# Two transformer layers on one core: the first head group of layer 0 laid out over TensorE's row groups, with q's split and the bias loads moved to other engines

## The reference

```python
x_norm = modulate(_ln(x), shift_a, scale_a)
qkv = x_norm @ W_qkv + b_qkv                 # b_qkv: 3 x 128
q, k, v = split(qkv)                         # 16 heads of 8 channels
attn_w = softmax(einsum('bhqd,bhkd->bhqk', q, k) * 8 ** -0.5)
attn_out = einsum('bhqk,bhkd->bhqd', attn_w, v)
...
x = x + gate_a * (attn_out @ W_proj + b_proj)
```

## Time and profile before

| | us |
|---|---|
| median of 3 executions | 492.45 |
| lowest and highest of them | 485.8, 495.92 |
| the profiled execution's own time | 483.93 |
| its span, first to last instruction | 482.2 |
| PE busy | 401.5 (83%) |
| DVE busy | 302.2 (63%) |
| ACT busy | 203.7 (42%) |
| POOL busy | 110.4 (23%) |

### The profile page before, as it was taken

One profiled execution on the slowest core, in us unless ns is written; L12 is line 12 of the kernel. 1 busy time (PEld: TensorE's weight loads), 2 busy tenths in 40 slices (PEclk: granted clock), 3 DMA queues, 4 the chain that ended last, 5 costly groups with the idle time before them and its releaser, 6 DMA issues.

```text
span 482.2 us, 9026 instructions
## 1 busy us (share of the span) xinstructions
PE 401.5 (83%) x3343; PEld 225.6 (47%) x3343; DVE 302.2 (63%) x1282; ACT 203.7 (42%) x302; POOL 110.4 (23%) x131
## 2 busy tenths in 40 slices
PE   3899999999998987989979897987674667675886
PEld 2436531223333225767655646773353444454454
DVE  4743663599999507466453725123988999997332
ACT  1120132466664774566723122431443555553411
POOL 5411030940001012000121400001434344444010
PEclk9855575699999999999989777555757777876989
DMA  7443144011000000000000000000000000000000
GB/s 194 33 152 93 50 145 133 16 50 52 2 2 1 2 0 1 2 2 1 1 0 1 3 3 6 5 3 0 2 1 2 1 2 0 2 1 1 1 24 22
DMA packets 11357, 12.22 MB, mean 25 GB/s; under 512 B 2335, under 2 KB 9713, under 8 KB 11313
## 3 DMA queue, kind: packets, MB, share of 16 engines
q1 hardware_dynamic: 10237, 10.96, 7.7%
q0 software_dynamic: 320, 0.34, 0.9%
q10 hardware_dynamic: 756, 0.34, 0.6%
HBM read 8.75 MB, written 2.62 MB: 24 GB/s over the span
## 4 chain that ended last, share of the span: by engine, by line
PE 58%; DVE 28%; ACT 6%; issue 5%; POOL 1%; DMA 1%; SPq 0%; ACTq 0%; DVEq 0%; POOLq 0%
PE psum L1515 5%; PE psum L1445 5%; PE psum L1483 5%; PE psum L1439 4%; DVE mx L1163 4%; PE psum L1468 3%; DVE left L1235 3%; DVE left L1242 3%; PE psum L1614 3%; PE psum L1306 3%; PE psum L1462 3%; PE psum L1498 3%; DVE top L1232 2%; PE psum L1526 2%; DVE top L1239 2%
## 5 line engine op out<-in xcount | busy, mean ns | idle before, releaser
L1163 DVE TENSOR_REDUCE mx<-psum 128x1 f32<-128x512 f32 x128 | 81.8, 684 | 38.3 <-PE psum L1445 22.4
L765 ACT ACTIVATE big<-psum 128x1024 f32<-128x1024 f32 x64 | 62.5, 1022 | 45.5 <-PE psum L1468 27.3
L575 POOL TENSOR_TENSOR rstd<-vareps,minus_half 128x4 f32<-128x4 f32 x12 | 12.2, 1020 | 191.2 <-DVE vareps L930 191.1
L1515 PE MATMUL psum<-kblk,qf 128*128 128x308 f32 x128 | 48.7, 515 | 1.1 <-DVE qf L1112 0.8
L1445 PE MATMUL psum<-KS,QS 72*128 72x512 bf16 x112 | 44.2, 429 | 3.4 <-DVE mx L1163 2.6
L1526 PE MATMUL psum<-ident,pr 128*77 128x128 f32 x256 | 39.1, 303 | 9.1 <-POOL pr L689 8.9
L1526 PEld LDWEIGHTS psum<-ident,pr 128*77 128x77 f32 x256 | 35.3, 170 | 17.3 <-POOL pr L689 12.2
L689 POOL TENSOR_TENSOR pr<-pr,early 128x616 f32<-128x616 f32 x16 | 23.9, 1493 | 56.5 <-ACT early L870 39.3
L1483 PE MATMUL psum<-big,V 128*9 128x512 f32 x256 | 36.0, 636 | 0.5 <-ACT big L765 0.5
L1538 PE MATMUL psum<-QS,vc 77*9 77x128 f32 x256 | 14.2, 348 | 23.2 <-ACT QS L880 23.1
L1468 PE MATMUL psum<-QS,KS 75*128 75x512 bf16 x112 | 33.1, 383 | 0.4
(11 more groups left out here) (205 smaller groups left out, 710.5 us busy)
## 6 DMA issues: line engine op xcount, KB each, us to landing
QS<-scr_q SPq DMA_DIRECT2D x7, 288.0 KB
KS<-scr_k SPq DMA_DIRECT2D x7, 288.0 KB
scr_q<-qp SPq DMA_DIRECT2D x2, 384.0 KB, 2.5
scr_k<-kp SPq DMA_DIRECT2D x2, 384.0 KB, 3.1
early<-in_L_xcond_w_ada_dram SPq DMA_DIRECT2D x1, 576.0 KB, 5.1
scr_k<-kp SPq DMA_DIRECT2D x2, 256.0 KB, 3.2
wmlp<-in_L_xcond_W_mlp_dram SPq DMA_DIRECT2D x2, 256.0 KB, 3.2
wm<-in_L_xcond_w_m_dram SPq DMA_DIRECT2D x1, 512.0 KB, 4.6
```

Source lines behind the costliest of these rows:

```text
L765: freed(act.activation(pT[:, u % 2, 1024 * half:1024 * (half + 1)], ps, ACT.Exp), "sT", 0, u, half)
L1163: freed(dve.tensor_reduce(mx[:, n % 3, NT * hh + q:NT * hh + q + 1], ps, AX_X, ALU.max), "max", t, q)
L1515: last = pe.matmul(ps[:, 512 * a:512 * a + HH // 2 * S], qf[:, b, i * P:(i + 1) * P], kb[:, c0:c0 + HH // 2 * S], start=True, stop=True)
```

## The change

- **Maxima of the first group.** A step t < 4 used to be head t with its four query tiles, all four from the same 8 partitions. Now it is query tile t of the four heads, each on its own row group and with all 32 rows of it. `mx` gets its columns in the order that fits. The scores of the group take all 32 rows too.
- **Blanks.** For this the rows behind the 8 channels must not disturb: `vecs` is zeroed first (DVE, with the semaphore s_vz on which the loads of the vectors wait), L1_b_qkv is moved to row 32 of it, and the 1 of row 8 is taken out of the q bias (two small memsets of `vecsF`).
- **q's parts.** DVE keeps one operation of five per batch (qf from PSUM). ACT makes the first and second bfloat16 part (`q_first`, `q_mid`), POOL the two differences. They stand in ACT's and POOL's lists between those of k.
- **Bias rows.** All ten `load_wide` copies are issued by ACT, one after the other, right behind half_tanh; none by POOL. There is one semaphore for all.
- **Order.** `mod_columns(0, 1)` moves from before the first maximum to behind "ln" of step 0, and its room from W0 ahead of the steps to the second turn of the W rooms; `ln_norm(0, 1)` moves from before Q0's copy to behind q's; `mod_out(0, 1)` moves from step 0 to step 1, `q_out(1)` from 1 to 2.

```diff
-EARLY_ROOMS = {"ln": (("W", ("lnT", 0, 1)),), ...
+EARLY_ROOMS = {"ln": (("W", ("lnT", 0, 1)), ("W", ("mods", 0, 1))), ...
-                  ("L1_b_ada", 9), ("L1_b_qkv", 3), ("L1_b_q", 1), ("L1_b_kv", 2), ("L1_b_m1", 8)):
+                  ("L1_b_ada", 9), ("L1_b_m1", 8), ("L1_b_q", 1), ("L1_b_kv", 2), ("L1_b_qkv", 3)):
+    _at = QUAD if _name == "L1_b_qkv" else _at
...
         def load_vecs(eng, loaded, *names):
+            eng.wait_ge(s_vz, 1)
...
@@ split_k (POOL)
                 pool.tensor_tensor(res[:, b, 1, :], kf[:, b, :], kp[:, b, 0, :], ALU.subtract).then_inc(s_kres[b], 1)
+                pool.wait_ge(s_qhi[b], 1)
+                pool.tensor_tensor(res[:, b, 0, :], qf[:, b, :], qp[:, b, 0, :], ALU.subtract).then_inc(s_qres[b], 1)
                 pool.wait_ge(s_kmid[b], 1)
                 pool.tensor_tensor(kp[:, b, 2, :], res[:, b, 1, :], kp[:, b, 1, :], ALU.subtract)\
                     .then_inc(s_parts[b], 1)
+                pool.wait_ge(s_qmid[b], 1)
+                pool.tensor_tensor(qp[:, b, 2, :], res[:, b, 0, :], qp[:, b, 1, :], ALU.subtract)\
+                    .then_inc(s_parts[b], 1)
...
-            load_wide(pool, 5, 6, 7, 8, 9)
...
-            load_wide(act, 0, 1, 2, 3, 4)
+            load_wide(act, *range(len(WIDE)))
...
@@ ACT, layer 0, each b
                         k_out(b)
+                        q_first(b)
                         k_mid(b)
+                        q_mid(b)
...
@@ q_out (DVE)
-                dve.tensor_scalar(qf[:, b, :], ps, cols_dh[:, c:c + 1], SCALE, ALU.add, ALU.mult)
-                freed(dve.tensor_scalar(qp[:, b, 0, :], ps, cols_dh[:, c:c + 1], SCALE, ALU.add, ALU.mult),
-                      "qkv", 0, b, "q")
-                wait_read(dve, "qkv", 0, b, "q")
-                dve.tensor_tensor(res[:, b, 0, :], qf[:, b, :], qp[:, b, 0, :], ALU.subtract).then_inc(s_qsplit[b], 1)
-                dve.wait_ge(s_qsplit[b], 1)
-                dve.tensor_copy(qp[:, b, 1, :], res[:, b, 0, :]).then_inc(s_qsplit[b], 1)
-                dve.wait_ge(s_qsplit[b], 2)
-                dve.tensor_tensor(qp[:, b, 2, :], res[:, b, 0, :], qp[:, b, 1, :], ALU.subtract)\
-                    .then_inc(s_parts[b], 1)
+                freed(dve.tensor_scalar(qf[:, b, :], ps, cols_dh[:, c:c + 1], SCALE, ALU.add, ALU.mult), "qkv", 0, b, "q")
...
             ln_stats(0, 1)
-            ln_norm(0, 1)
...
                     q_out(0)
+                    ln_norm(0, 1)
...
-                                freed(dve.tensor_reduce(mx[:, n % 3, NT * hh + q:NT * hh + q + 1], ps, AX_X, ALU.max),
-                                      "max", t, q)
+                                at = NT * q + hh if n == 0 else NT * hh + q
+                                freed(dve.tensor_reduce(mx[:, n % 3, at:at + 1], ps, AX_X, ALU.max), "max", t, q)
...
             qk(0)
-            mod_columns(0, 1)
...
@@ max_L0, j < G
-                    filled(pe.matmul(ps, Q0[QUAD * h:QUAD * h + D, q * P:(q + 1) * P], K0[QUAD * h:QUAD * h + D, :],
+                    filled(pe.matmul(ps, Q0[QUAD * q:QUAD * q + QUAD, j * P:(j + 1) * P], K0[QUAD * q:QUAD * q + QUAD, :],
...
@@ sT_L0, n == 0
-                        last = pe.matmul(ps[:, t * N:(t + 1) * N], K0[r0:r0 + DV, kt * P:(kt + 1) * P], Q0[r0:r0 + DV, :],
+                        last = pe.matmul(ps[:, t * N:(t + 1) * N], K0[r0:r0 + QUAD, kt * P:(kt + 1) * P], Q0[r0:r0 + QUAD, :],
...
                             if item == "ln":
                                 ln_T(0, 1)
+                                mod_columns(0, 1)
```

More of the change, by code:

```diff
@@ L57 @@
          6: ("gates2",)}
-EARLY_ROOMS = {"ln": (("W", ("lnT", 0, 1)),), "qk": (("M0", ("qkv", 0, 1, "q")), ("W", ("qkv", 0, 1, "k"))),
+EARLY_ROOMS = {"ln": (("W", ("lnT", 0, 1)), ("W", ("mods", 0, 1))), "qk": (("M0", ("qkv", 0, 1, "q")), ("W", ("qkv", 0, 1, "k"))),
                "v0": (("W", ("qkv", 0, 0, "v")),), "v1": (("W", ("qkv", 0, 1, "v")),),
@@ L115, in rooms_in_turns @@
     use("M1", "qkv", 0, 0, "k")
-    use("W0", "mods", 0, 1)
     for layer in range(2):
@@ L366, in build @@
         s_first = sem("first_vecs_loaded")
-        s_wide = [sem("wide_of_L0_loaded"), sem("wide_of_L1_loaded")]
+        s_wide = sem("wide_loaded")
         s_wrows = sem("row_weights_ready")
@@ L389, in build @@
         s_hat = each("ln_normed")
-        s_qsplit = each("q_split_steps")
+        s_qhi = each("q_first_part_ready")
+        s_qres = each("q_rest_ready")
+        s_qmid = each("q_second_part_ready")
         s_kres = each("k_rest_ready")
@@ L410, in build @@
         s_fz = sem("row_group_blanks_set")
+        s_vz = sem("vecs_zeroed")
         s_vwz = sem("window_v_blanks_set")
@@ L445, in load_wide @@
                 src = ins[name[:2] + "_xcond" + name[2:]].rearrange("(r c) -> r c", c=C)[r:r + 1, :]
-                eng.dma_start(wide[:, n, :], src.broadcast_to([P, C])).then_inc(s_wide[n // 5], 16)
+                eng.dma_start(wide[:, n, :], src.broadcast_to([P, C])).then_inc(s_wide, 16)
         def parts_to_scratch(sp, b):
@@ L616, in gate_outputs @@
                                                    gates[:, gk, :], ALU.mult).then_inc(s_gw[n], 1)
-                            pool.wait_ge(s_wide[row // 5], 16 * 5)
+                            pool.wait_ge(s_wide, 16 * len(WIDE))
                             pool.tensor_tensor(gb[:, n, b, :], wide[:, row, :], gates[:, gk, :], ALU.mult)\
@@ L737, in rows_k_out, with q_first @@
                 freed(ins_, "rows", "k")
+            def q_first(b):
+                wait_read(act, "qkv", 0, b, "q")
+                act.activation(qp[:, b, 0, :], qf[:, b, :], ACT.Copy).then_inc(s_qhi[b], 1)
             def k_mid(b):
@@ L742, in k_mid, with q_mid @@
                 act.activation(kp[:, b, 1, :], res[:, b, 1, :], ACT.Copy).then_inc(s_kmid[b], 1)
+            def q_mid(b):
+                act.wait_ge(s_qres[b], 1)
+                act.activation(qp[:, b, 1, :], res[:, b, 0, :], ACT.Copy).then_inc(s_qmid[b], 1)
             def window_k_out(b):
@@ L978, in v_out @@
                     dve.wait_ge(s_ones, 2)
-                    dve.wait_ge(s_wide[0], 16 * 5)
-                    dve.wait_ge(s_wide[1], 16 * 5)
+                    dve.wait_ge(s_wide, 16 * len(WIDE))
                 for i in range(NT):
@@ L1040, in mod_out @@
                 dve.tensor_scalar(scales, scales, 1.0, None, ALU.add).then_inc(s_mod, 1)
+            dve.memset(vecs[:, :], 0.0).then_inc(s_vz, 1)
             dve.memset(negbig[:, :], -BIG).then_inc(s_nb, 1)
@@ L1046, in _ @@
             dve.memset(vecsF[:, :, :, DV:QUAD], 0.0).then_inc(s_fz, 1)
+            dve.wait_ge(s_fz, 1)
+            for name in ("L0_b_qkv", "L1_b_qkv"):
+                dve.memset(vecsF[VECS[name]:VECS[name] + 1, :, :, D:DV], 0.0).then_inc(s_fz, 1)
             dve.wait_ge(s_blank, 1)
@@ L1173, in _ @@
                             ctx_stats()
+                        if t == 1:
                             mod_out(0, 1)
-                        if t == 1:
+                        if t == 2:
                             q_out(1)
-                        if t == 2:
                             ctx_norm()
@@ L1362, in vec_columns @@
                 pe.wait_ge(s_dh, 2)
-                pe.wait_ge(s_fz, 2)
+                pe.wait_ge(s_fz, 4)
                 ps = open_room(pe, "vecs")
```

## The result

The changed kernel takes 464.89 us (median of 4, 462.83 to 468.88) against 491.72 us of the kernel before (4 runs, 485.8 to 495.92): ratio 0.950, interval 0.938 to 0.962. The forecast was 477 (463 to 489). A second set on another chip (a_again) gave 462.97 against 487.09: 0.955, interval 0.950 to 0.960. The changed kernel's profile is of its longest execution, 468.88 us. The ratios leave out every execution more than 1.5% above the fastest of its kernel on its chip, the medians keep them, and where a kernel's executions differ much the two part (a_rows9 has 2 of its 10 executions in its ratio).

A forecast was written before the change was run, and what follows sets the result against it. It took PE's own work, mostly at the lower clock in the first 95 us, as the bound. Savings of 8.6 us up to step 4 and 7 in the scores, 15.6 off the median 492.45, gave 477 us (463 to 489).

The forecast's parts named there:

- Maxima side by side: First group's maxima, steps 1 to 3: products on different row groups overlap, three rooms limiting them; 6.3 us saved.
- Start: Up to step 1: later hT of batch 0 against less work before the first maxima; 0.8 us saved, 0 to 1.3.
- hT behind q_mid: Batch 1's hT waits in ACT's list behind q_mid: cost 0, or 0.9 us if step 1 runs at full clock.
- Jobs between: v and the eighteen small products behind step 2, partly at full clock: 1.5 us saved together.
- To the begin of step 4: Sum of maxima, start and jobs between: 8.6 us saved, bounds 3.7 and 15.
- The scores: First group's scores: extra rows bring full clock back for a bit more than half the stretch; 7 us saved.
- The base: Starting time: savings summed on the profiled 483.93 us execution, then taken off 492.45, the median of the other three.
- Rival 2: Clock stays high from the first maxima on, through the scores: 27 us saved, 465 us; chance 0.13.
- Rival 1: Clock in the scores stays as it is, only steps get shorter: 8.6 us or less saved, 484; chance 0.27.
- Rivals 3 and 4: 3: full clock returns later, slower, 505 us, chance 0.04. 4: row groups do not overlap, 492 us, chance 0.06.
- the marks I named: Signs expected in the changed profile: overlapping maxima, earlier transposes, times of hT and scratch write, scores' end, full clock.

The follow-up runs named there:

- a_again: The changed kernel, unchanged, measured and profiled again on another chip: 462.97 us, ratio 0.955.
- a_rows9: The changed kernel with 8 rows in the first group's maxima and 9 in its scores, heads still side by side: median 486.17 us, ratio 0.987.
- a_serial: The changed kernel with each maxima step again one head with four query tiles, sharing one row group of 32 rows: 469.96 us, ratio 0.962.
- a_order: The changed kernel with all ten bias rows loaded from SP's queue and batch 1's hT ahead of k_mid and q_mid: 463.61 us, ratio 0.957.
- b_scores32: The kernel before with 32 rows in place of 9 in the first group's scores, nothing else: 470.1 us, ratio 0.967.
- a_scores16: The changed kernel with 16 rows in place of 32 in the first group's scores: 483.57 us, ratio 0.994.
- b_again: The kernel before, unchanged, profiled a second time: 490.45 us.
- a_win32: The changed kernel with 32 rows in place of 8 and 9 in layer 1's window maxima and scores: 459.46 us, ratio 0.947.

## Why the prediction was right

The range held the time near its low end (a_again's median, 462.97, is just below it), the direction and the place were right, and the likeliest size was too small: 477 against 464.9. Between the two profiles the sum said 15.6 us and 15.0 came. That agreement is luck: the scores gave 5.2 more than forecast, and everything else, start to end, 5.8 less. Step by step:

- **Maxima side by side: right.** Forecast 4.5 us at 1.2 GHz and 2.7 at 2.4; measured 4.9 (39.12 to 44.04) and 3.0 (30.52 to 33.55). a_serial gives back 7.12, 4.10, 7.12. The three rooms do set the step. The three that ran together took 2.08 us at 1.2 GHz where single file would take 5.3; the wait and the fourth add 2.8. The 3.07-fold speedup of four at once that the Trainium skill gives (TensorE: Matmul & The Clock Gate, Part 3: Packing small matmuls) did not come about here: 7.12 to 4.9 is 1.45.
- **Start: the sum right, its parts not.** ACT's issues were slower than the pitch I took (one of 0.73, one of 0.55), so hT came at 11.68, not 11.0; step 1 still began 1.3 us earlier, with the full clock on from 16.4 to 26.6 (in the kernel before it was at 0.54 from 21 to 23.75).
- **hT behind q_mid: right as a mechanism, taken too small.** I had 0 in the sum and 0.9 for a fast step 1. Step 1 was fast, hT was ready at 27.17, and PE waited 1.8. a_order takes the wait away.
- **Jobs between: wrong.** I had 1.5 for v and the small products, behind a shorter step 2, at full clock. They took as long as before (1.87 and 3.77 us): the clock fell at 33.5, as v began.
- **To the begin of step 4: 8.6 forecast, 7.1 measured.** Steps 4 to 6, where I had nothing, lost 2.6: in the kernel before, the clock was full from 58.8, for their last 5 us; in the changed one from 57.4, 1.8 us before their end. The clock rose at nearly the same time, but PE had got further by then, so less of this work ran at full clock.
- **The scores: the mis-sized term.** I took "the clock is back at 2.4 GHz for a bit more than half of the stretch: 7". It was at 2.4 all of it, and 12.2 came back, the upper bound. b_scores32 and a_rows9 show that it is the rows, a_scores16 that half of them is not enough.
- **The base: a second mis-sized term.** For a like execution I forecast 468, and the profiled one took 468.9 against 483.9. But that sets the fastest of the four executions then known against the slowest of the changed kernel's four. The sum held everything behind 92.9 unchanged, while the kernel before can come to full clock 10 us later and lose it again (b_again, 6.0 us), as a_rows9 and a_scores16 did, and its times spread over 480 to 499. The changed one enters the later groups at full clock and spreads over 462 to 469. The two spans before, 482.2 and 488.6, and the two after, 467.2 and 462.3, are 15.0 to 26.3 apart, and the medians 24 and 27. How often each pattern comes is not known, as the other executions have no profile.
- **Rivals.** Rival 2 named 465 and had 0.13; its scores came true, its first steps did not (0.50 from 33.5 to 57.4). So its number is luck too. One of its reasons was a misreading: the earlier trace rows prints the full level in the first slice, but there the row does not fit the products, for batch 0's first four records took 3.66 us from 10.95 on (3.75 from 12.60 on in the changed kernel), the pace of 1.2 GHz. Rival 1, with the rule of the Trainium skill (TensorE: Matmul & The Clock Gate, Part 1: The HAM clock gate) that the clock follows how busy PE is, is refuted: PE is 100% busy in a_scores16's 27.3 us at 0.50, and 99% in the changed kernel's 16.3 us at 1.00. Rivals 3 and 4 did not occur.

Of the marks I named, the scratch write began at 28.08 (27.5 forecast), batch 1's transposes at 21.04 (before 21), and the first group's scores ended at 75.5 (77 to 84).

## What to carry to other kernels

Look at the granted clock of a stretch beside its busy share: a PE that is always busy at 1.2 GHz with few rows at work may be made faster by giving it rows of zeros, which cost no time here (a step of maxima in single file takes 7.12 us with 8 rows and with 32). Products of few rows can run side by side on different row groups, and here the number of PSUM rooms decided how many did. Profile the old kernel twice before taking a sum from it, when its executions differ by more than the terms.

## What the hardware showed that was not expected

- The same stretch of products, all of PE's time busy: 27.1 us with 9 rows, 27.3 with 16, 16.3 with 32.
- In layer 1's windows (64 columns of weights, 64 moved) 32 rows brought 10.2 us at full clock into a stretch of 44 at half (a_win32).
- The kernel before had two patterns of the clock behind 92 us with the same instructions, 6 us apart. The slower one was not seen in any of the ten profiles with 32 rows in the first group's scores.
